# The kv and m chain of batches 0 to 2 and the q projections of tiles 0 to 3 run as guests among the K tiles of phase one; the first steps of phase two are regrouped

## The reference

```python
xn = layernorm(x)
q, k, v = elu(xn @ Wq) + 1, elu(xn @ Wk) + 1, xn @ Wv      # in heads
z  = einsum("bhnd,bhd->bhn", q, k.sum(tokens)) + 1e-6
kv = einsum("bhnd,bhne->bhde", k, v)
x  = x + (einsum("bhnd,bhde->bhne", q, kv) / z) @ Wo + bo
h  = square(relu(layernorm(x) @ W_fc.T))
y  = h @ W_proj.T
# five steps of a leaky integrate-and-fire neuron on y; out = spikes / 5
x  = x + mean_of_spikes(y)
```

## Time and profile before

| what | value |
|---|---|
| median of 3 runs | 1070.83 us (1070.75 to 1071.7) |
| profiled execution | 1072.46 us, its span 1070.7 us |
| PE busy | 1031.0 us, 96% |
| DVE busy | 947.7 us, 89% |
| ACT, POOL busy | 723.0 us, 652.9 us |
| granted TensorE clock | 0.998 of full speed |
| last g_tile of phase one ends | 356.8 us |

### The profile page before, as it was taken

One profiled execution on the slowest core, in us unless ns is written; L12 is line 12 of the kernel. 1 busy time (PEld: TensorE's weight loads), 2 busy tenths in 40 slices (PEclk: granted clock), 3 DMA queues, 4 the chain that ended last, 5 costly groups with the idle time before them and its releaser, 6 DMA issues.

```text
span 1070.7 us, 18777 instructions
## 1 busy us (share of the span) xinstructions
PE 1031.0 (96%) x6596; PEld 615.9 (58%) x6596; DVE 947.7 (89%) x1871; ACT 723.0 (68%) x1209; POOL 652.9 (61%) x389
## 2 busy tenths in 40 slices
PE   8999999999999887899999999999999999999997
PEld 4444444444444455556666676766666676666676
DVE  7888888988877789999999999999999999999956
ACT  6777787777777456676666666767667676766662
POOL 3444444444445354787878777787877778777732
PEclk9999999999999999999999999999999999999999
DMA  5445523334232244354454544445545444544511
GB/s 137 124 132 129 133 74 99 87 87 114 64 104 69 47 88 103 86 104 100 99 120 103 104 109 99 100 99 104 107 106 100 99 99 102 102 108 91 85 40 35
DMA packets 263086, 104.15 MB, mean 97 GB/s; under 512 B 217296, under 2 KB 260432, under 8 KB 262992
## 3 DMA queue, kind: packets, MB, share of 16 engines
q1 hardware_dynamic: 262992, 102.96, 42.7%
HBM read 33.69 MB, written 16.79 MB: 47 GB/s over the span
## 4 chain that ended last, share of the span: by engine, by line
PE 80%; DVE 14%; ACT 2%; DMA 2%; issue 1%; POOL 1%; SPq 1%; DVEq 0%; ACTq 0%; POOLq 0%
PE proj L431 27%; PE acc L561 14%; PE acc L539 14%; PE acc L457 13%; PE acc L526 12%; DVE feat L926 2%; DVE xn L782 2%; DVE zsum L929 1%; DVE feat L792 1%; DVE spikes L903 1%; DVE m_all L887 1%; DMA xT<-xnat 1%; DVE xnat L787 1%; DVE bn L764 1%; DMA qT<-feat 1%
## 5 line engine op out<-in xcount | busy, mean ns | idle before, releaser
L1019 POOL TENSOR_TENSOR h<-h_f,h 128x512 f16<-128x512 f32 x128 | 145.7, 1160 | 158.6 <-ACT h L729 158.6
L1013 POOL TENSOR_TENSOR feat<-feat 128x1024 f16<-128x1024 f32 x64 | 190.6, 2979 | 11.7 <-ACT feat L707 11.7
L526 PE MATMUL acc<-m_all,qT 128*128 128x256 f16 x1536 | 178.2, 273 | 10.1 <-DMA qT<-feat 5.4
L431 PE MATMUL proj<-xn2T,xT 128*128 128x512 f16 x768 | 177.6, 381 | 6.3 <-DVE feat L792 3.1
L561 PE MATMUL acc<-wpT,h 128*128 128x256 f16 x1536 | 177.8, 273 | 2.1 <-DVE spikes L903 2.1
L457 PE MATMUL acc<-feat,xnat 128*128 128x512 f16 x768 | 176.5, 379 | 1.5 <-DVE feat L830 1.5
L431 PE MATMUL proj<-wq,xT 128*128 128x512 f16 x768 | 176.3, 379 | 0.0
L539 PE MATMUL acc<-xn2T,wfcT 128*128 128x512 f16 x768 | 176.2, 379 | 0.0
L716 ACT ACTIVATE h_r<-acc 128x512 f32<-128x512 f32 x128 | 75.7, 596 | 148.6 <-PE acc L539 148.4
L526 PEld LDWEIGHTS acc<-m_all,qT 128*128 128x128 f16 x1536 | 149.4, 98 | 42.6 <-DMA qT<-feat 9.9
L561 PEld LDWEIGHTS acc<-wpT,h 128*128 128x128 f16 x1536 | 149.8, 98 | 21.9 <-DVE spikes L903 3.7
(11 more groups left out here) (62 smaller groups left out, 1449.1 us busy)
## 6 DMA issues: line engine op xcount, KB each, us to landing
x_t<-in_L_attn_x_dram SPq DMA_DIRECT2D x128, 128.0 KB, 2.3
xT_spill<-xT SPq DMA_DIRECT2D x64, 128.0 KB, 2.0
xT<-xT_spill SPq DMA_DIRECT2D x64, 128.0 KB, 2.3
out_dram<-out_t SPq DMA_DIRECT2D x64, 128.0 KB, 2.1
ks_all<-ks_rows SPq DMA_DIRECT2D x4, 512.0 KB, 4.4
m_all<-in_L_attn_Wk_dram SPq DMA_DIRECT2D x4, 256.0 KB, 4.5
xT<-xnat SPq DMA_TRANSPOSE x64, 2.4
m_all<-in_L_ffn_W_fc_dram SPq DMA_DIRECT2D x4, 256.0 KB, 3.4
```

What stands on the lines that cost most here:

```text
L431: mm = pe.matmul(proj[:, slot, half * HALF:(half + 1) * HALF], xT[:, u, left * C2 + c2, :], w[:, right, c2, half * HALF:(half + 1) * HALF] ...
L526: mm = pe.matmul(acc[:, 0, 0:D], qT[:, n % 4, left * PAIRS + j, :], m_at(n // BT, right, j), start=(i == 1), stop=(i == PAIRS * len(PRODUC ...
L1013: pool.tensor_tensor(feat16[:, n % 2, LO, :], feat[:, n % 2, :], feat16[:, n % 2, HI, :], ALU.subtract).then_inc(q_lo, 1)
L1019: pool.tensor_tensor(h[:, c % 2, LO, f, :], h_f[:, k % 4, :], h[:, c % 2, HI, f, :], ALU.subtract).then_inc(h_lo, 1)
```

## The change

**Phase one** gets a table of 13 guests. After K tile n+1 PE does the guest of n, if there is one: a chain job of batch 0, 1 or 2, or the q projection of tile 0, 1, 2 or 3. A guest takes a slot of `proj` in turn with the K tiles, so kv, k-sum and m no longer use `acc` for these batches, and each user waits for the user two places earlier (`wait_slot`). The operations on the other engines stand at fixed distances behind: for a chain job one or two tiles later, for a q tile n its elu at +2, times k-sum at +3, reduce at +4, reciprocal at +5 (DVE), `normalise_q` in two halves at +4 and +5 and `q_lo_tile` in four quarters at +8 to +11 (POOL), `turn_q` at +13 (SP). Behind a guest the exp and the elu of the next K tile come earlier in ACT's and DVE's lists. The k-sum job and `take_ks` move from the batch's end to the kv guest. The splitting of the weights moves forward (one piece per tile at 5 to 15 and 18 instead of every second tile at 6 to 12, 22 to 28 and 38 to 44), and so do weight loads and transposes. POOL's memset is gone, the first tile of a batch is copied instead of added.

**Phase two** keeps only the chain of batch 3 (steps 3 to 5) and starts with q tile 4. The tiles of a step come from functions now: `o_tile` 0 to 3 in steps 3, 4, 5, 5; first feed-forward product of tiles 0 to 3 in steps 8 to 11 instead of 9 to 12; second one in 12 to 15 instead of 13 to 16. From tile 4 on all stand in the same steps as before, so step 12 has no `f1`, step 16 no `f2`, and step 6 no PE work.

```diff
-        KV_AT = {2 * b + 1: b for b in range(B)}
-        M_AT = {2 * b + 2: b for b in range(B)}
+        GUESTS = {20: ("kv", 0, 0), 22: ("m", 0, 0), 24: ("m", 0, 1), 26: ("q", 0), 30: ("q", 1),
+                  36: ("kv", 1, 0), 38: ("m", 1, 0), 40: ("m", 1, 1), 43: ("q", 2), 46: ("q", 3),
+                  52: ("kv", 2, 0), 54: ("m", 2, 0), 56: ("m", 2, 1)}
...
+        def o_step(n):
+            return {0: 3, 1: 4, 2: 5, 3: 5}.get(n, n + 3)
+        def f1_step(n):
+            return n + 8 if n < 4 else n + 9
+        def f2_step(n):
+            return n + 12 if n < 4 else n + 13
+        STEPS = range(3, TILES + 16)
...
+            def guest_job(kind, *which):
+                if kind == "q":
+                    q_tile(*which)
+                elif kind == "kv":
+                    wait_slot(pe, kind, *which)
...
+                    ks_job(which[0])
+                    kv_job(which[0])
+                else:
+                    wait_slot(pe, kind, *which)
...
+                    m_job(*which)
...
                 if live(n + 1):
                     k_tile(n + 1)
-                if n > 1 and n % BT == 1:
-                    ks_job(n // BT - 1)
+                if n in GUESTS:
+                    guest_job(*GUESTS[n])
                 if n:
                     g_tile(n - 1)
...
+                if q_guest(n, 5) is not None:
+                    q_inverse(q_guest(n, 5))
                 if 1 < n < TILES and n % BT == 1:
                     copy_g(n // BT - 1)
+                if live(n) and n - 1 in GUESTS:
+                    k_elu_tile(n)
                 if live(n + 2):
                     normalise_a(n + 2)
                 if n:
                     k_lo_tile(n - 1)
+                if q_guest(n, 3) is not None:
+                    q_times_ks(q_guest(n, 3))
...
-                if 1 < n < TILES and n % BT == 1:
-                    take_ks(n // BT - 1)
-                if live(n):
-                    dve.wait_ge(k_exp, n + 1)
-                    elu_plus_one(n % 2, k_feat(n)).then_inc(k_elu, 1)
+                if live(n) and n - 1 not in GUESTS:
+                    k_elu_tile(n)
+                if q_guest(n, 4) is not None:
+                    q_reduce(q_guest(n, 4))
```

More of the change, by code:

```diff
@@ new lines, in m_job @@
+            def m_job(b, i):
+                pe.wait_ge(chain_free, through("kv", b, 0))
+                for qq in range(2):
+                    for s in range(2):
+                        for side in range(2):
+                            slot = 4 * s + 2 * i + qq
+                            own = slice(side * DH, (side + 1) * DH)
+                            mm = pe.matmul(m_half(b, i, side, qq)[s * DH:(s + 1) * DH, :],
+                                           kvT[own, b % 2, slot * DH:(slot + 1) * DH], wo[own, slot, :],
+                                           start=True, stop=True)
+                mm.then_inc(chain_full, 1)
@@ L676, in _ @@
                     xn_hi_a(n + 2)
-                if live(n):
+                if live(n) and n - 1 not in GUESTS:
                     k_exp_tile(n)
+                kind, *which = GUESTS.get(n - 1, (None,))
+                if kind == "q":
+                    q_exp_tile(*which)
+                elif kind == "m":
+                    m_hi_job(*which)
                 if live(n + 3):
@@ L849, in _ @@
             for n in range(TILES + 1):
+                kind, *which = GUESTS.get(n - 2, (None,))
+                if kind == "kv":
+                    take_kv(which[0])
+                    take_ks(which[0])
+                elif kind == "m":
+                    m_lo_job(*which)
+                elif kind == "q":
+                    q_elu_tile(*which)
+                if q_guest(n, 5) is not None:
+                    q_eps(q_guest(n, 5))
                 if live(n + 2):
@@ new lines, in _ @@
+            dve.wait_ge(k_added, TILES)
+            for t in STEPS:
+                spiking = at(f2_step, t - 1)
+                for k in range(5):
+                    if t > EARLY and live(t - 1) and not (k == 0 and t - 1 == EARLY):
+                        Q_STEPS[k](t - 1)
+                    for n in spiking:
+                        spike_step(n, k)
+                for n in spiking:
+                    write_out(n)
+                normal, fresh = at(o_step, t - 1), at(o_step, t)
+                for n in normal:
+                    newton(ln2, n)
+                    normalise(ln2, x2_at(n), n)
+                for n in fresh[:1]:
+                    residual(n)
+                for n in normal:
+                    xn_lo(ln2, n)
+                for n in fresh[:1]:
+                    stats_b(n)
+                if t == 3:
+                    take_ks(B - 1)
+                    take_kv(B - 1)
+                for n in fresh[1:]:
+                    residual(n)
+                    stats_b(n)
+                if t in (4, 5):
+                    m_lo_job(B - 1, t - 4)
```

526 lines of the change are left out of this document (285 added, 241 removed).

## The result

The changed kernel takes 1074.74 us (median of 6 runs, 1073.96 to 1076.21) where the kernel before took 1070.88 (6 runs, 1070.6 to 1071.7). The ratio is 1.0037, 95% interval 1.0024 to 1.005: slower by 3.9 us, where 3.8 less was forecast. A later set of runs gave 1.0028 (1.0017 to 1.0039). The profiled execution took 1074.56, its span is 1072.8.

The account below looks back on a forecast made before the run. DVE was taken to bound the handover, PE the rest. Idle-time terms -7.2 - 3.7 - 0.9 + 5.2 + 2.2 + 0.6 = -3.8 gave span 1066.9, median 1067.0 us; range 1061 to 1075.5, likeliest case 1063.5 to 1068.7.

Parts of the forecast that it names:

- Part 2, the batch ends: After batches 0 to 2: K tile waits behind `take_ks` go, 3.7 us, and one wait for a transposed xT, 0.9.
- Part 3, the guests: Phase one: each of 13 guests starts 0.35 to 0.4 us late, waiting for an elu; costs 5.2 us, bounds nothing to 15.9.
- Rival 1: Phase one: guests are dear, PE pays 1.2 us at each of 13; 1077.4 at worst, 1075 likely; chance 0.18.
- q's tails (2.2): Phase one: DVE's times-k-sum and reduce make K tiles behind each q guest 0.3 + 0.25 us late; costs 2.2.
- SP's stores (0.6): Phase one, tile 39: a q transpose and four k-sum stores stand in one tile of SP's queue; costs 0.6 us.
- Part 1, the handover: Phase one to two: handover 29.9 us shorter, 22.7 of it moved work, net gain 7.2; second f2 at 89.7, step 13 at 83.8.
- The waits named: PE's remaining handover waits: elu of q tiles 5 and 6 (3.9, 2.8 us), o tile 3 (1.8), second f2 (6.0).
- PE has no idle time before either: Behind the second f2: later f2 keep their old distance and PE has no idle time, so no cost counted.
- Rival 2: Phase one: POOL's 24 pieces stop DVE, 15 us of DVE time, half reaching PE, +7.5: 1074.5; chance 0.05.
- Rival 3: Handover doesn't get shorter, +7.2: 1074.2, chance 0.07; with part of it 1070 to 1072, chance 0.18.

Follow-up runs that it names:

- before_batch_end: Kernel before, at batch ends ACT and DVE make xn's halves before copying G, `take_ks` behind the K tile's elu; 1066.05 us, ratio 0.9949.
- guest_behind_g: Changed kernel with PE's guest of tile n behind g tile n-1 instead of ahead of it; 1068.2 us, ratio 0.9969.
- q_retimed: Changed kernel with the q guests moved from tiles 26, 30, 43, 46 to 27, 31, 43, 45; 1073.14 us, ratio 1.0011.
- after_waits: Changed kernel plus two long-fulfilled waits on PE in each of tiles 2 to 46; 1073.19 us, ratio 1.0019.
- elu5_early: order_fixed with DVE's elu of q tile 5 moved from step 6 to step 5, behind the residual; 1064.31 us, ratio 0.9927.
- after_filler: Changed kernel plus unread filler matmuls on PE, 15 in step 6 and 30 in step 12; 1072.52 us, ratio 1.001.
- before_waits: Kernel before plus two long-fulfilled waits on PE in each of tiles 2 to 46; 1071.28 us, ratio 0.9996.
- elu5_filler: elu5_early plus 30 unread filler matmuls of 256 columns on PE in step 12; 1062.76 us, ratio 0.9918.
- order_fixed: guest_behind_g with xn's halves before G's copies at batch ends (ACT, DVE), q's times-k-sum behind the K tile's elu; 1065.73 us, ratio 0.9946.
- elu5_waits: elu5_early plus two long-fulfilled waits on PE in each of tiles 2 to 46, no filler; 1064.51 us, ratio 0.9937.
- batch_end_waits: before_batch_end plus two long-fulfilled waits on PE in each of tiles 2 to 46; 1065.77 us, ratio 0.9947.
- before_batch_end_2: Same kernel as before_batch_end, run again in a later set against the kernel before; 1067.15 us, ratio 0.9958.

## Why the prediction was wrong

- **Part 2, the batch ends: the step that failed.** It took 3.7 + 0.9 off because `take_ks` left, and asked only who had been last. Next in DVE's list stood `copy_g`, which waits for the batch's last g tile, and the q guests' times-k-sum at 33 and 49, the very tiles of batch end 1 and 2. The waits moved to xT (0.40, 1.13, 1.13) and g tiles (3 x 0.25), 3.4 in place of 4.0. Of 4.6 foreseen 0.6 came, 4.0 less than counted, which alone is more than the 3.4 by which phase one was off; before_batch_end shows the 5.4 that were there.
- **Part 3, the guests: right mechanism, size off.** 0.38 for an undisturbed guest was foreseen as 0.35 to 0.4. But five of the 13 had something late besides (gaps of 0.55 to 1.18), and the total was about 7.6, not 5.2. The distances between the starts of K tiles (5.18 us where no guest stands between) divide it more exactly: the 13 guests take 32.6 in the changed kernel and 25.9 in guest_behind_g, so the order costs 6.7; and an m guest takes 1.22 even without a wait, where the sum had 1.05, which is 1.0 for the six. Rival 1's mechanism (DVE late at guests) held at the five; the mean over all is 0.5 to 0.6, not its 1.2. The error that mattered more was to take the order as given: one g tile further back there is nothing to pay.
- **q's tails (2.2) and SP's stores (0.6)** did not appear where they were put. No K tile behind a q guest waited for xT but at the batch ends. There the times-k-sum is likely what makes the waits at batch ends 1 and 2 0.7 longer than at batch end 0, 1.5 in all; q_retimed, with no times-k-sum on a batch end, had 0.11 and none. That phase one was off by only 3.4 is partly luck: these terms and the loss at the batch ends had opposite signs.
- **Part 1, the handover.** 91.14 against 89.7: step 13 began at 85.1, not 83.8. The net gain was 5.7, not 7.2. The waits named (elu of q tiles 5 and 6, o tile 3, second f2) are those of the trace, 4.0 for 3.9, 1.2 for 2.8, 1.9 for 1.8, 1.1 for 6.0; the transposed q took 7.4, which was not foreseen.
- **Behind it, 1.1.** "PE has no idle time before either" held for before only. With one tile more ahead of it, f2 waits 0.89 for the spikes at 527.97.
- **Rival 2** was 1 to 2 us, not 7.5. **Rival 3** fell: the handover did get shorter, from 127.38 to 91.14, where 30.5 is moved work.
- **The clock** had no term. PE's longest wait in the old handover was 1.9, in the new 4.0. In the changed kernel's profile the slow product behind it cost nothing; in after_waits, elu5_early and after_filler slow products cost 0.7 to 1.7.
- Sum: 3.4 of the 5.9 by which the spans miss the forecast come from phase one, 1.5 from the handover, 1.1 from behind (rounded). The other 1.8 up to the medians belong to no stage with certainty: the profiled execution of the kernel before took 1.6 more than its median, and it has the half clock at its start, 1.0 against before_waits; how often its other executions have it isn't shown.

The fastest kernel here, elu5_filler, is 0.8% below the kernel before (0.9918); the batch-end order alone gives 0.9949 and 0.9958, and between kernels with and without the moved chains and q tiles, both orders right and the packet in like place, lie 0.3 us (order_fixed, before_batch_end), 1.3 us (elu5_waits, batch_end_waits) and 2.8 us (elu5_early, before_batch_end_2). The last two pairs also have the moved elu. That the moved chains and q tiles are worth anything by themselves is thus not shown; the order at the batch ends is.

## What to carry to other kernels

When an operation that ended a wait is taken away, follow the same engine's list to the next one that waits for the same event; the gain is the distance to that one, not the length of the wait. Work inserted between two saturated products belongs behind the product that gives its buffer's last reader time, and the seam is worth trying in both orders before the cost is called a price of the idea. And where a stage of the profile keeps its length to 0.03 us over seven kernels, the engine that sets it in them is known; the kernels in which the length changes (91.88, 92.82) show where that cover ends. Two profiles are compared from the first point at which they run alike, since here their starts alone differed by more than a microsecond.

## What was not expected of the hardware

- One instruction-queue packet of 0.02 MB in the midst of DMA transposes lengthened the time from issue to landing, 4.4 to 4.9 us without it, to 5.9 to 6.1 us. 45 to 90 more instructions on PE, in phase one or the handover, moved it away, so a kernel that merely has more or fewer instructions can differ by up to 1.3 us in one wait; that is a third of the difference studied here.
- Half clock behind some waits of PE in each profile of the changed structure, and in one of the old structure (before_batch_end_2), with products of 4.0 to 5.3 instead of 2.75. In the handover DVE's list hid up to 4.46 behind the wait for the transposed q; a product of 5.30 there cost 0.7 to 0.9 us, and one of 4.45 at o tile 3, for which DVE waits, cost 1.7, as much as it was longer.
- At the start the product behind a wait of 1.7 to 2.3 us took 4.0 to 4.5 in ten profiles and 2.76 in eight, and K tile 17 started 0.5 to 1.7 us apart by it.
